# A load of keys or rows is issued only when the load four before it has landed

## The reference, cut to what matters

```
x = x + xattn(layernorm(x), ctx)
  Sim  = (h @ w1)[:, None] + (ctx @ w2)[None, :] + (h * w3) @ ctx.T + b     # 128 x 12544
  A    = softmax(Sim, axis=1)
  hq   = A @ ctx                                                            # 128 x 256
  bar  = softmax(max(Sim, axis=1)) @ h
  out  = concat([h, hq, h * hq, h * bar]) @ W_qv + b_qv
x = x + attn(layernorm(x))      # q, k, v projections, rope, (q k^T) v without softmax, Wo
x = x + ffn(layernorm(x))       # token shift, relu squared, sigmoid gate
```

## Time and profile before

| | us |
|---|---|
| median of 3 runs | 113.17 (112.5 to 113.83) |
| the profiled execution's own time | 112.1 |
| span of the profiled execution | 110.3 |
| PE busy | 105.1 (95%) |
| DVE busy | 93.1 (84%) |
| ACT busy | 82.4 (75%) |
| POOL busy | 29.3 (27%) |
| granted TensorE clock | 1.0 throughout |
| HBM read | 29.57 MB |

### The profile page before, as it was taken

The page is one execution under the profiler, slowest core; times in us unless marked ns, Lnnn a source line. Parts: engine busy times, 40 slices in busy tenths (PEclk is TensorE's granted clock), DMA queues, the critical chain, the costliest instruction groups (busy, mean ns, idle before and its releaser), DMA issues.

```text
span 110.3 us, 1855 instructions
## 1 busy us (share of the span) xinstructions
PE 105.1 (95%) x582; PEld 86.4 (78%) x583; DVE 93.1 (84%) x152; ACT 82.4 (75%) x171; POOL 29.3 (27%) x47
## 2 busy tenths in 40 slices
PE   5999999999999999999999999999999998998890
PEld 2368768588858888899899999989898997887680
DVE  1478999999998998999999999999999847674352
ACT  5067668899979989999999899988976725903450
POOL 2239200444043314233242424286330000200100
PEclk9999999999999999999999999999999999999999
DMA  2999999999999999999999999960000000000001
GB/s 72 367 406 423 416 422 422 416 422 422 409 420 417 418 415 423 417 420 442 442 389 423 415 422 425 406 260 0 3 0 0 0 6 0 0 0 0 6 3 48
DMA packets 8220, 29.82 MB, mean 270 GB/s; under 512 B 1042, under 2 KB 1298, under 8 KB 8082
## 3 DMA queue, kind: packets, MB, share of 16 engines
q1 hardware_dynamic: 8064, 29.69, 66.3%
q10 hardware_dynamic: 146, 0.01, 0.1%
HBM read 29.57 MB, written 0.13 MB: 269 GB/s over the span
## 4 chain that ended last, share of the span: by engine, by line
PE 94%; DVE 1%; issue 1%; ACT 1%; DVEq 0%; ACTq 0%
PE mixed_ps L997 18%; PE scores_ps L968 10%; PE mixed_ps L999 9%; PE scores_ps L940 8%; PE scores_ps L944 8%; PE scores_ps L954 8%; PE scores_ps L925 7%; PE scores_ps L910 4%; PE scores_ps L979 3%; PE scores_ps L1090 2%; PE mixed_ps L1142 2%; PE side_ps L1016 1%; PE scores_ps L1155 1%; PE side_ps L1133 1%; PE scores_ps L1016 1%; PE scores_ps L1125 1%
## 5 line engine op out<-in xcount | busy, mean ns | idle before, releaser
L698 DVE TENSOR_TENSOR pair<-raw,pair 128x1024 fp32r<-128x1024 f32 (+2 forms) x42 | 49.0, 1183 | 1.3 <-ACT pair L488 1.0
L488 ACT ACTIVATE pair<-raw 128x512 fp32r<-128x512 f32 (+1 forms) x42 | 34.5, 820 | 3.8 <-DMA raw<-keys_dram 3.4
L997 PE MATMUL mixed_ps<-pair,turned_high 128*128 128x512 f32 x84 | 32.3, 418 | 0.0
L999 PE MATMUL mixed_ps<-pair,turned_low 128*128 128x256 f32 x84 | 23.6, 281 | 0.0
L463 POOL CAST pair<-raw 128x512 fp32r<-128x512 f32 x22 | 13.6, 619 | 27.3 <-DVE pair L698 23.1
L997 PEld LDWEIGHTS mixed_ps<-pair,turned_high 128*128 128x128 f32 x84 | 15.8, 188 | 2.8
L520 ACT ACTIVATE turned_high<-scores_ps 128x512 fp32r<-128x512 f32 (+1 forms) x23 | 13.4, 584 | 4.0 <-PE scores_ps L968 4.0
L721 DVE TENSOR_SCALAR_CACHE_REDUCE neg_scores<-scores_ps,neg_max 128x1024 f32<-128x1024 f32 (+1 forms) x13 | 15.8, 1216 | 0.2
L999 PEld LDWEIGHTS mixed_ps<-pair,turned_low 128*128 128x128 f32 x84 | 16.0, 190 | 0.0
L728 DVE TENSOR_TENSOR turned_low<-scores_ps,turned_high 128x512 fp32r<-128x512 f32 (+1 forms) x23 | 15.3, 667 | 0.2 <-ACT turned_high L520 0.2
L968 PE MATMUL scores_ps<-ident,neg_scores 128*128 128x128 f32 x98 | 14.6, 272 | 0.0
(11 more groups left out here) (189 smaller groups left out, 130.6 us busy)
## 6 DMA issues: line engine op xcount, KB each, us to landing
raw<-keys_dram SPq DMA_DIRECT2D x24, 512.0 KB, 10.0
raw<-rows_dram SPq DMA_DIRECT2D x24, 512.0 KB, 9.2
w<-weights_dram SPq DMA_DIRECT2D x1, 1792.0 KB, 9.9
w<-weights_dram SPq DMA_DIRECT2D x2, 512.0 KB, 10.4
const<-const_dram SPq DMA_DIRECT2D x1, 832.0 KB, 11.5
raw<-keys_last_dram SPq DMA_DIRECT2D x1, 256.0 KB, 10.2
raw<-rows_last_dram SPq DMA_DIRECT2D x1, 256.0 KB, 6.8
x_sb<-x_dram SPq DMA_DIRECT2D x1, 128.0 KB, 2.2
```

What stands on the lines that cost most here:

```text
L488: nc.scalar.activation(pair[:, use % PAIR_BUFS, 0, 0:columns], raw[:, slot(item), 0:columns], ACT.Copy)\
L698: nc.vector.tensor_tensor(out=pair[:, use % PAIR_BUFS, 1, 0:columns], in0=raw[:, slot(item), 0:columns], in1=pair[:, use % PAIR_BUFS, 0, 0 ...
L997: nc.tensor.matmul(mixed_ps[:, :].rearrange("p (h d) -> p h d", h=2), probs_high, both[:, :, t * D:(t + 1) * D], start=(k == EARLY and t = ...
L999: last = nc.tensor.matmul(mixed_ps[:, 0:D], probs_low, rows_tile(high, t), start=False, stop=(k == LATE - 1 and end))
```

## The change

There is a new constant `IN_FLIGHT` = 4, and `wait_for_slot` begins with one more wait. From item 4 on SP waits until item n - 4 has landed, and then, from item 10 on, for the slot as before. Since `wait_for_slot` serves keys and rows and the items are numbered through, the first rows count the last keys. The loads of weights, constants, x, vec and bias don't go through `wait_for_slot`: they are neither held back nor counted.

```diff
 RING = 10
+IN_FLIGHT = 4
 PAIR_BUFS = 5
...
         def _(sp):
             def wait_for_slot(item):
 
+                if item >= IN_FLIGHT:
+                    landed = item - IN_FLIGHT
+                    sp.wait_ge(loaded[slot(landed)], loads(landed))
                 before = item - RING
                 if before < 0:
                     return
```

## The result

The changed kernel took 113.97 us in the median of 6 runs (113.37 to 115.7); the kernel before, run beside it, took 112.59 (112.22 to 113.83, 6 runs). The ratio is 1.0124, with a 95% interval from 1.0082 to 1.0167. That is 1.4 us more, inside the range of 112.2 to 114.3 us, but on the side that I had given a chance of 0.10. The profiled execution took 113.37 us with a span of 111.5, 1.2 us over that of before. Medians are of all runs, but each ratio leaves out the runs that lie more than 1.5% above the fastest of the same kernel, one of the six here; TensorE's granted clock fell to 1.2 GHz near the end of some runs (for 3.4 us from 103.5 us on in the trace of e2_depth5), and most of those runs still count.

A forecast was written before the change was run, and what follows sets the result against it. PE was taken to bound the kernel, with DMA just ahead in the keys. All terms were 0: 110.3 us of span plus 1.8 around it, 112.1, or 113.2 on the scale of the median, range 112.2 to 114.3 us.

The forecast's parts named there:

- the side that I had given a chance of 0.10: Whole kernel: slower by over 1%, a chance of 0.10, for most of the case that four loads are too few.
- The waits: On SP, 46 of 50 items get a wait; bounds for one already met were 0 and 0.1 us, taken as 0.
- The weights and the later rows: Weights keep their place in the order, and slot waits already held SP in the rows; cost 0 for each.
- The rows stage: From 48.5 to 88 us, DMA at a share of 0.65, so a small loss there would be made up; cost 0.
- The reserve of 1.3 us: Steady state of loads: 3.75 us of queued transfers, less 2.35 for a fresh load and 0.1 reaction, leaves 1.3 us.
- row 11's 5.2 us: Row 11, issued at 47.7 us behind four loads, landed 5.2 us later with engines full; taken as four transfers, cost 0.
- They lose a lead: Loads from 30 us on: faster DMA engines running dry cost 0, since the slowest keeps its 3.75 us of transfers.
- the signs set down beforehand: Forecast wrong if the DMA share falls before 46 us; expected 418 GB/s from 7 to 42 us, ACT's key waits near 3.4.
- My first rival: Keys 4 to 19: each load takes 1.35 us instead of 1.25, end moves 1.3 us to 114.5; chance 0.09.
- Nothing there is later than its data needs to be: Rows: slot waits stay behind the new wait, slots free each 1.7 us, slower than 1.25; cost 0.
- The forecast of no cost: Whole kernel: keys issued 5 us later, landings where they were, time 113.2 us; chance 0.84.
- rows 6 to 8: Profile lines: x landed after 2.2 us, key 0 after 3.6, row 11 after 5.2, engines full at 420 GB/s.

The follow-up runs named there:

- e2_depth5: The changed kernel with IN_FLIGHT = 5 in place of 4; 112.35 us, ratio 1.0001 to the kernel before.
- e1: The changed kernel with IN_FLIGHT = 10 in place of 4, so each wait is already met; 112.18 us, ratio 0.999 to the kernel before.
- e9: The changed kernel with the gate for rows 4 to 24 alone, keys and rows 0 to 3 as before; 112.51 us, ratio 1.0027.
- e11: The changed kernel with IN_FLIGHT = 1 in place of 4, each load alone in the queue; 195.32 us in one run.
- e10: The changed kernel with IN_FLIGHT = 2 in place of 4; 139.68 us in one run.
- e4: The changed kernel with IN_FLIGHT = 3 in place of 4; 124.37 us, ratio 1.102 to the kernel before.
- e5: The changed kernel with the gate for the keys alone, rows waiting only for their slots; 113.34 us, ratio 1.0045 to the kernel before.
- e8: The changed kernel with the gate beginning at item 8 instead of item 4; 113.98 us, ratio 1.014 to the kernel before.
- e6: The changed kernel with the gate for the rows alone, keys going out as before; 113.70 us, ratio 1.0116 to the kernel before.

## Why the prediction was right and wrong

**What held.** The waits cost nothing (e1). Loads go out later and mostly land on time: 416 GB/s from 8 to 32 us, and a median of 5.2 us for rows. The weights and the later rows cost nothing, or little (e9). The rows stage didn't pay anything back.

**The reserve of 1.3 us failed.** It was worked out from key 0, with x alone ahead of it. That agrees with what a load alone takes (3.2 us, e11), but loads with others behind and ahead take 1.0 to 1.3 us longer (e10, e4). The nearest row was another: row 11's 5.2 us. I read it as four transfers of 1.25 us and took it as evidence of ease; in fact four transfers and the loaded round trip were the same number, and row 11 stood on the edge. A row at the edge can't tell slack from none.

**"They lose a lead" failed.** I wrote that faster engines that run dry cost nothing, since the slowest sets every landing. In the kernel after, key 20 landed at 26.9 + 6.2 = 33.1 us and key 21 at 28.2 + 7.4 = 35.6, 2.4 us apart where 1.25 were due:

```profile
L405 SPq DMA_DIRECT2D raw<-keys_dram x1: 328/328/328, 26.9 to 26.9; - x1
DMA to landing us min/median/max: 6.2/6.2/6.2
...
L405 SPq DMA_DIRECT2D raw<-keys_dram x1: 328/328/328, 28.2 to 28.2; - x1
DMA to landing us min/median/max: 7.4/7.4/7.4
```

That held row 0 back until 35.6 us, with keys 22, 23 and the half load ahead of it, and the share then fell to 0.81. The engines that had run dry were the late ones for row 1: it landed 2.1 us behind row 0. The kernel before had such a fallen-back engine too, and its queue of eight hid it. With a deep queue the lags of different engines hide behind each other; a gate on whole loads adds them up. This reading fits the traces of e5 to e8, but the views don't give one engine's landings, so it is argued, not shown.

**The path was not the one that I named.** By the signs set down beforehand the account behind the forecast is wrong: the DMA share fell, to 0.81, before 46 us; from 7 to 42 us the engines moved 398 GB/s instead of 418; ACT's waits for keys grew from 3.4 to 4.7 us. My first rival, "four are not enough", had the right sign and nearly the right size: 1.3 us, and 1.4 were measured. It lost them evenly, 0.10 us a load, at key 19 through DVE. The measured loss came in one stretch, from 36 to 44 us, and reached PE at row 2 through ACT. I had dismissed the rows with "Nothing there is later than its data needs to be", without pricing what row 2 has to spare: landed at 41.7, taken by ACT at 42.3, so 0.6 us. A landing 1.6 us later leaves 1.0 us, which is what PE lost there.

**The chances.** That 113.97 us lies in the range of 112.2 to 114.3 us is luck in part. The forecast of no cost, with its 0.84, did not come; the range held because I had stretched it to the edge of the first rival, and because the kernel before took 112.59 us this time: 1.0124 times the 113.17 us that the range was built on would be 114.6, outside it. I gave that rival 0.09 with rows 6 to 8 against it. Rows 6 spoke of an almost empty queue, and rows 7 and 8 fitted the rival as well as the forecast. The page of the Trainium skill ("DMA: Bandwidth & Descriptors", Latency and other measured facts) puts a DMA's fixed cost at some 2 us and HBM's access latency at 2 us at high load. The first agrees with e11, 3.2 - 1.25 = 1.95 us; with the second no run here can be compared: e4 shows 5.0 - 3.75 = 1.25 us over the transfers, and not how much of it is HBM's.

**What stays open.** Why loads in company take 1.0 to 1.3 us longer; what holds one engine back, a fetch of instructions over the same engines being a candidate, since one packet of 16 KB on the instruction queue began at 32.8 us in after, just ahead of key 21's late landing; and how the 1.2% divide between keys and rows, which intervals of about 0.5% don't tell. For that candidate the traces hold more. All eleven of the table have such a packet between 28.1 and 34.3 us, and in ten of them a load lands 2.0 to 2.8 us after it that is 0.4 to 1.5 us late, counted from the load ahead of it and its own 1.25 us of transfer; in the kernel before it is that of the weights behind key 18, after a packet at 28.4 us. With one load in flight, a packet at 105.3 us fell into the flight of row 7, which took 4.3 us where the median is 3.3 us. No run takes the packet away, so it stays a likely source and no more, and it doesn't explain the late row 1 of e6, which has no such packet near.

## What to carry to other kernels

To ask how many loads must be in flight, measure the round trip under load, not that of a first load in an empty queue; if the number of loads times one transfer only equals it, there is no reserve, and here one more load brought the time back (e2). A throughput that is full on average says nothing of the one load that an engine meets ahead of the critical engine's work: look up what that load has to spare. Such a load may be better placed behind that work in the list of the engine that takes it: here that gave back 0.67 us in one trace, while the times don't show it clearly.

## What the runs showed of the hardware

For 512 KB loads on one queue, with 1, 2, 3, 4, 5 and 10 allowed in flight, keys took 3.2, 4.3, 5.0, 5.6, 7.0 and 10.1 us to land in the median. From 7 to 42 us they ran at 161, 262, 329, 398, 415 and 418 GB/s together with the weights. The times were 195.3, 139.7, 124.4, 114.0, 112.4 and 112.2 us. I had expected the knee at three.
